# Attention kernel on one core: the parts of a projected chunk go through DRAM, and a batch's weighted sums all stand ahead of the next batch's first value tile

## The reference

```python
q, k, v = X @ Wq, X @ Wk, X @ Wv            # heads of 64; rotary embedding on q and k
att = softmax(causal(50 * tanh(q @ k.T * 256**-0.5 / 50)))
x = layernorm(X + (att @ v) @ Wo)
y = per_token_int8(x) @ weight.T * in_scale * w_scale + bias   # as float16
return layernorm(x + y)
```

## Time and profile before

| | us |
|---|---|
| median of 3 runs | 1504.92 (1504.58 to 1505.42) |
| the profiled execution, its own time | 1501.25 |
| its span, first to last instruction | 1499.3 |
| TensorE (PE) busy | 1322.7 |
| VectorE (DVE) busy | 1096.8 |
| ScalarE (ACT) busy | 849.1 |
| GpSimd (POOL) busy | 380.8 |

### The profile page before, as it was taken

One profiled execution on the slowest core, in us unless ns is written; L12 is line 12 of the kernel. 1 busy time (PEld: TensorE's weight loads), 2 busy tenths in 40 slices (PEclk: granted clock), 3 DMA queues, 4 the chain that ended last, 5 costly groups with the idle time before them and its releaser, 6 DMA issues.

```text
span 1499.3 us, 17504 instructions
## 1 busy us (share of the span) xinstructions
PE 1322.7 (88%) x5824; PEld 963.7 (64%) x5840; DVE 1096.8 (73%) x1367; ACT 849.1 (57%) x952; POOL 380.8 (25%) x448
## 2 busy tenths in 40 slices
PE   6479999978988999897886999999599799999695
PEld 5357777656655777675664777767476477777463
DVE  4369888863677888885486888888258788888485
ACT  4167687752236777764223777687123577779232
POOL 2231111102552111110265112111036312111165
PEclk9789999989988999998998999999799899999896
DMA  7766445474513454547341454446642154343541
GB/s 280 261 205 160 103 129 144 113 211 123 156 50 87 115 139 109 155 96 244 95 133 47 98 137 117 103 144 186 181 123 78 56 137 103 102 110 103 149 109 42
DMA packets 120765, 196.22 MB, mean 131 GB/s; under 512 B 26466, under 2 KB 68964, under 8 KB 116836
## 3 DMA queue, kind: packets, MB, share of 16 engines
q1 hardware_dynamic: 114916, 185.14, 44.2%
q10 hardware_dynamic: 5760, 9.97, 2.0%
HBM read 89.39 MB, written 38.54 MB: 85 GB/s over the span
## 4 chain that ended last, share of the span: by engine, by line
PE 62%; DVE 10%; DMA 9%; SPq 7%; issue 5%; ACT 3%; POOL 3%; ACTq 1%; DVEq 0%; POOLq 0%
PE ps L735 21%; PE ps L655 15%; PE ps L709 14%; PE ps L777 6%; PE ps L677 4%; SPq L427 4%; DMA y_scratch<-sums 3%; DMA rows<-r_scratch 2%; DVE prob_hi L1109 1%; ACT probs L914 1%; DVE stats L1195 1%; DVE probs L1174 1%; DMA qk<-work_r 1%; DMA r_scratch<-inverse 1%; POOL rstd L1332 1%
## 5 line engine op out<-in xcount | busy, mean ns | idle before, releaser
L735 PE MATMUL ps<-prob_hi,v 128*65 128x512 f32 (+3 forms) x1280 | 415.1, 374 | 3.3 <-DVE prob_lo L1113 3.3
L914 ACT ACTIVATE probs<-ps 128x1024 f32<-128x1024 f32 x288 | 293.6, 1020 | 161.9 <-PE ps L709 159.2
L709 PE MATMUL ps<-qk 128*128 128x512 f32 (+1 forms) x1280 | 322.9, 379 | 54.2 <-DMA qk<-work_r 28.4
L1113 DVE TENSOR_TENSOR prob_lo<-probs,prob_hi 128x1024 fp32r<-128x1024 f32 x288 | 360.1, 1250 | 9.9
L1317 POOL TENSOR_SCALAR_AFFINE_SELECT probs<-probs 128x256 f32<-128x256 f32 (+1 forms) x192 | 145.3, 765 | 808.0 <-ACT probs L919 808.0
L919 ACT ACTIVATE probs<-probs 128x1024 f32<-128x1024 f32 x288 | 305.6, 1061 | 8.8
L709 PEld LDWEIGHTS ps<-qk 128*128 128x128 f32 x1280 | 230.1, 193 | 116.9 <-ACT probs L914 27.9
L655 PE MATMUL ps<-xT,w_ring 128*128 128x512 f32 x1152 | 293.5, 399 | 10.0 <-DVE xT L1051 8.0
L1109 DVE CAST prob_hi<-probs 128x1024 fp32r<-128x1024 f32 x288 | 206.3, 716 | 118.5 <-POOL probs L1317 69.6
L655 PEld LDWEIGHTS ps<-xT,w_ring 128*128 128x128 f32 x1152 | 219.6, 193 | 58.3 <-DVE xT L1051 9.3
L735 PE MATMUL ps<-prob_lo,v 128*65 128x512 f32 (+1 forms) x640 | 239.2, 374 | 0.0
(11 more groups left out here) (77 smaller groups left out, 1042.9 us busy)
## 6 DMA issues: line engine op xcount, KB each, us to landing
qk<-work_r SPq DMA_DIRECT2D x256, 128.0 KB, 2.3
qk<-work_r SPq DMA_DIRECT2D x488, 64.0 KB, 2.0
y_scratch<-sums SPq DMA_DIRECT2D x128, 130.0 KB
wo<-wo_scratch SPq DMA_DIRECT2D x8, 2048.0 KB, 7.8
y_raw<-y_scratch SPq DMA_DIRECT2D x64, 256.0 KB, 4.1
w_ring<-w_scratch SPq DMA_DIRECT2D x15, 1024.0 KB, 5.8
x_raw<-X_T SPq DMA_DIRECT2D x16, 512.0 KB, 5.1
x_in<-X SPq DMA_DIRECT2D x32, 256.0 KB, 2.9
```

Of the source, the lines that this page charges most:

```text
L709: mm = nc.tensor.matmul(scores[:, g % 2, col:col + REP * w].rearrange("p (h q) -> p h q", h=REP), qk[:, n % 2, i, 2 + part, keys], qk[:, n ...
L735: mm = nc.tensor.matmul(sums_ps[:, :, GQ - w:GQ], v[:, kt, v0:v0 + width], p[:, at, col:col + REP * w].rearrange("p (h q) -> p h q", h=REP ...
L914: nc.scalar.activation(probs[:, prob_place(g), :], scores[:, g % 2, :], ACT.Tanh, scale=SCORE_SCALE / SOFTCAP).then_inc(capped, 1)
L1113: nc.vector.tensor_tensor(prob_lo[:, prob_place(g), :], probs[:, prob_place(g), :], prob_hi[:, hi_place(g), :].bitcast(F32), ALU.subtract) ...
```

## The change

A part of a chunk is written by one DMA of 128 partitions (`send`) to a new DRAM tensor, and read from there into `qk` (`take`) by 4 DMAs for k and 2 for each half of q, all issued by SP. `rope_read` waits for the send alone. For m > 1 the high part is taken right behind the low part's send, the low part one step later; for m = 1 all takes stand at steps 15 to 17 of unit 0. `qk` has a new inner order, all q ahead of all k, so `score` waits for both head pairs' parts together. The weighted sums of steps 69 to 71 stand ahead of value tile 0; value tile 1 stands behind `spread_rows` of tile 0. The value weights' last two quarters are loaded at step 14. `wo` is loaded after a batch's last score, its low half behind `load_rows` of tile 1; in the last batch both halves are loaded at steps 1 and 2 of its last unit, into the place of xT. ScalarE issues no puts.

```diff
--- before
+++ after
@@ -101,6 +101,8 @@
+    chunk_scratch = nc.dram_tensor("chunk_scratch", [2, 3, 2, P, T], F32, kind="Internal").ap()
...
@@ -123,8 +125,9 @@
-        qk = sb("qk", [P, 2, 2, 4, T], F32R)
-        wo = over("wo", "qk", [P, 2, KO, C], F32R, skip=32 * KB)
+        qk = sb("qk", [P, 2, 2 * REP + 4, T], F32R)
+        wo_first = over("wo", "qk", [P, 2, KO, C], F32R, skip=32 * KB)
+        wo_last = over("wo_last", "xT", [P, 2, KO, C], F32R)
...
@@ -309,8 +313,11 @@
-        def puts_upto(m):
+        def k_puts_upto(m):
...
+        def q_puts_upto(m):
+            return 64 * (m // 2 + 1)
...
@@ -324,9 +331,9 @@
-        def wait_put(eng, m, x):
-            for i in range(2):
-                eng.wait_ge(k_put[m % 2][i] if x == 0 else q_put[m % 2][x - 1][i], puts_upto(m))
+        def wait_sent(eng, m, x):
+            for low in range(2):
+                eng.wait_ge(chunk_sent[place_of(m, x)][low], 16 * ((3 * m + x) // 2 + 1))
...
@@ -334,6 +341,9 @@
+        def wo_of(b):
+            return wo_last if b == B - 1 else wo_first
...
@@ -395,37 +405,6 @@
-        def put(eng, m, x, low):
-            eng.wait_ge(rope_lo if low else rope_hi, chunks_upto(m, x))
-            if m == 0:
-                eng.wait_ge(w_stored[1], 16)
-                eng.wait_ge(w_stored[2], 16)
-            if m == 1:
-                eng.wait_ge(wo_stored, 32)
-            if m >= 2:
-                eng.wait_ge(scored, unit_scored(m - 2))
-            if m % UB == 1 and m > 1:
-                eng.wait_ge(o_done, rows_upto(m // UB - 1, NT - 1))
-            buf = qk[:, m % 2, :, :, :]
-            for i in range(2):
-                if x == 0:
-                    for half in range(2):
-                        src = work_r[64 * half + 32 * i:64 * half + 32 * (i + 1), place_of(m, x), 1 - low, :].bitcast(F32)
-                        for copy in range(2):
-                            r0 = 64 * copy + 32 * half
-                            eng.dma_start(buf[r0:r0 + 32, i, 2 + low, :].bitcast(F32), src
-                                         ).then_inc(k_put[m % 2][i], 16)
-                else:
-                    cols = slice((x - 1) * HT, x * HT)
-                    for r in range(REP):
-                        h = REP * i + r
-                        for half in range(2):
-                            src = work_r[32 * h:32 * (h + 1), place_of(m, x), 1 - low, half * HT:(half + 1) * HT].bitcast(F32)
-                            r0 = 64 * low + 32 * half
-                            eng.dma_start(buf[r0:r0 + 32, i, r, cols].bitcast(F32), src
-                                         ).then_inc(q_put[m % 2][x - 1][i], 16)
...
@@ -486,6 +465,13 @@
+            def load_wo(b, part):
+                if b == B - 1:
+                    sp.wait_ge(projected, chunks_upto(U - 1, 2))
+                sp.dma_start(wo_of(b)[:, part, :, :].rearrange("p k n -> p (k n)").bitcast(F32),
+                             wo_scratch[:, part * KO * C:(part + 1) * KO * C]
+                             ).then_inc((wo_hi_loaded, wo_lo_loaded)[part], 16)
...
@@ -494,6 +480,40 @@
                 cols = slice(part * KC * C // 2, (part + 1) * KC * C // 2)
                 sp.dma_start(w_v[:, :, :, :].rearrange("p w k n -> p (w k n)")[:, cols].bitcast(F32),
                              wv_scratch[:, cols]).then_inc(wv_loaded, 16)
+
+
+            def send(m, x, low):
+                sp.wait_ge(rope_lo if low else rope_hi, chunks_upto(m, x))
+                if m >= 2 and x == 0:
+                    sp.wait_ge(k_put[m % 2], k_puts_upto(m - 2))
+                elif m >= 2:
+                    sp.wait_ge(q_put[m % 2][x - 1], q_puts_upto(m - 2))
+                sp.dma_start(chunk_scratch[m % 2, x, low], work_r[:, place_of(m, x), 1 - low, :].bitcast(F32)
+                             ).then_inc(chunk_sent[place_of(m, x)][low], 16)
+
+            def take(m, x, low):
+                sp.wait_ge(chunk_sent[place_of(m, x)][low], 16 * ((3 * m + x) // 2 + 1))
+                if m == 0:
+                    sp.wait_ge(w_stored[1], 16)
+                    sp.wait_ge(w_stored[2], 16)
+                if m == 1:
+                    sp.wait_ge(wo_stored, 32)
+                if m >= 2:
+                    sp.wait_ge(scored, unit_scored(m - 2))
+                if m % UB == 1 and m > 1:
+                    sp.wait_ge(o_done, rows_upto(m // UB - 1, NT - 1))
+                for half in range(2):
+                    if x == 0:
+                        src = chunk_scratch[m % 2, 0, low, 64 * half:64 * (half + 1), :].rearrange("(i d) n -> d i n", i=2)
+                        for copy in range(2):
+                            r0 = 64 * copy + 32 * half
+                            sp.dma_start(qk[r0:r0 + 32, m % 2, 2 * REP + 2 * low:2 * REP + 2 * low + 2, :].bitcast(F32), src
+                                         ).then_inc(k_put[m % 2], 16)
+                    else:
+                        src = chunk_scratch[m % 2, x, low, :, half * HT:(half + 1) * HT].rearrange("(h d) n -> d h n", d=32)
+                        r0 = 64 * low + 32 * half
+                        sp.dma_start(qk[r0:r0 + 32, m % 2, 0:2 * REP, (x - 1) * HT:x * HT].bitcast(F32), src
+                                     ).then_inc(q_put[m % 2][x - 1], 16)
             def put_sums(b, j, c):
                 n = groups_upto(b, j, c)
@@ -533,11 +553,13 @@
             sp.wait_ge(w_lo_done, 1)
             sp.dma_start(wo_raw[:, :, :], Wo.rearrange("(k p) n -> p k n", p=P)).then_inc(wo_raw_in, 16)
             for x in range(3):
-                put(sp, 0, x, 0)
+                send(0, x, 0)
                 if x == 0:
                     sp.wait_ge(projected, chunks_upto(0, 0))
                     load_wk(1)
-                put(sp, 0, x, 1)
+                send(0, x, 1)
+                take(0, x, 0)
+                take(0, x, 1)
             sp.wait_ge(projected, chunks_upto(0, 2))
             load_wq(1)
@@ -552,21 +574,31 @@
                         if m == 1 and s == 5:
                             sp.wait_ge(wo_hi_done, 4)
                             sp.dma_start(wo_scratch[:, 0:KO * C],
-                                         wo[:, 0, :, :].rearrange("p k n -> p (k n)").bitcast(F32)
+                                         wo_first[:, 0, :, :].rearrange("p k n -> p (k n)").bitcast(F32)
                                          ).then_inc(wo_stored, 16)
                             sp.wait_ge(wo_lo_done, 4)
                             sp.dma_start(wo_scratch[:, KO * C:2 * KO * C],
-                                         wo[:, 1, :, :].rearrange("p k n -> p (k n)").bitcast(F32)
+                                         wo_first[:, 1, :, :].rearrange("p k n -> p (k n)").bitcast(F32)
                                          ).then_inc(wo_stored, 16)
                         if s == 3 and m % UB and m + 1 < U:
                             sp.wait_ge(projected, chunks_upto(m, 0))
                             load_wk(m + 1)
                         if u == UB - 1 and s == 14:
                             load_div(b, 0)
+                            if b + 1 < B:
+                                load_wv(b + 1, 2)
+                                load_wv(b + 1, 3)
                         if at := chunk_at(b, u, s, turns(u, 5, 10, 14)):
-                            put(sp, *at, 0)
-                        if (at := chunk_at(b, u, s, turns(u, 6, 11, 15))) and at != (UB * b + UB, 2):
-                            put(sp, *at, 1)
+                            send(*at, 0)
+                        if at := chunk_at(b, u, s, turns(u, 6, 11, 15)):
+                            send(*at, 1)
+                            if m > 1:
+                                take(*at, 0)
+                        if (at := chunk_at(b, u, s, turns(u, 7, 12, 16))) and m > 1:
+                            take(*at, 1)
+                        if m == 1 and s >= 15:
+                            take(1, s - 15, 0)
+                            take(1, s - 15, 1)
                         if s == turns(u, 0, 0, 12)[2] and m < U:
                             sp.wait_ge(projected, chunks_upto(m, 2))
@@ -582,32 +614,28 @@
                             load_x_turned(b + 1, s - 12)
                             if s == 15:
                                 load_wq(m + 1)
-                        if u == UB - 1 and m < U and s in (14, 15):
-                            load_wv(b + 1, s - 12)
-                        if u == UB - 1 and s == 11:
-                            sp.wait_ge(scored, scores_upto(b, u * 2 * NS + NS - 1))
-                            sp.dma_start(wo[:, 0, :, :].rearrange("p k n -> p (k n)").bitcast(F32),
-                                         wo_scratch[:, 0:KO * C]).then_inc(wo_hi_loaded, 16)
+                        if b == B - 1 and u == UB - 1 and s in (1, 2):
+                            load_wo(b, s - 1)
                         if u == UB - 1 and s == 17:
```

(35 more changed lines are left out.)

9 lines of the change are left out of this document (5 added, 4 removed).

## The result

The changed kernel takes 1532.4 us (median of 4 runs, 1528.98 to 1534.38) against 1505.17 for the kernel before (1504.58 to 1507.07): a ratio of 1.0176, interval 1.0152 to 1.02. **It is slower by 27 us; the forecast was 16 us faster.** Its profiled execution took 1528.98 us and is compared with the 1501.25 of before; the spans are 1526.9 and 1499.3.

The account below looks back on a forecast made before the run. PE bounds the attention stretches, so time could come only from its stops. +12.1 (unit 1) - 7 (start) - 16 (boundaries) - 5.2 (last batch) = -16.1 us: 1485.1 profiled, 1489 as median; range 1475 to 1503.

Parts of the forecast that it names:

- Prices: Assumed costs: 0.63 us per back-to-back SP issue, 2.6 us for a send's landing, 2.9 us for a take's.
- Part 1: Attention stretches: chunk 2's low part reaches step 2 of the next unit with 2.1 us cover; worth 0.
- the round trip misses the deadline: Slower rival: at step 2 of the next unit, 11 times, landings exceed the 2.1 us cover: 23 us, 1512; chance 0.1.
- Part 2: Unit 1, once: late takes stop PE for 9.9 us, plus 2.2 at low clock; loss 12.1, ends 6 and 15.
- Part 3: Start of the kernel: chunks 1 and 2 arrive earlier for PE's first scores; gain 7 us, ends 4 and 9.
- Part 4: Three batch boundaries: SP's chain to the reciprocal loads moves 4.3 us earlier; gain 5.3 us each, 16 in all.
- the boundary gives nothing: Rival: wo's low half 5 us late, or the send slow under value-weight loads; boundaries give 0 to 2 each, 1502; chance 0.12.
- Part 5: End of the last batch: wo loaded early, so the second reciprocal load comes 5.2 us earlier; ends 3 and 6.
- the boundary gives all: Rival: SP's chain does not hold spread_rows(1), so 9.21 + 2.2 us goes at each boundary: 1471; chance 0.08.
- The bounds of the sum: Whole kernel: 1478 (start 9, boundaries 7 each less what cannot coincide) to 1499 (unit 1 at 15, boundaries at 3).

Follow-up runs that it names:

- extra sends: Kernel before, with every part also sent to DRAM (96 sends, 50 MB, unread) ahead of its puts, VectorE waiting for the landing: 1534.32 us, ratio 1.0187.
- the copies: Kernel before, with 84 copies of 512 KB DRAM to DRAM ahead of the puts, which only the next such copy waits for: 1517.31 us, ratio 1.0081.
- the two best kernels: Kernel before, direct puts, rest of change, SP's reciprocals earlier: 1472.18 us; changed kernel with unit 1's takes, last units' loads, reciprocals and wo's low half reordered: 1490.81 us.

## Why the prediction was wrong

**The step that failed is Prices.** It charged a take 0.63 us on SP and 2.9 us of landing, from rows of other transfers, and let takes overlap without limit. The runs put 1.17 us of all DMA engines in its place, and landings of up to 9.34 us for a send and 10.74 for a take where other transfers are ahead. The row to see it in was there: eight of k's puts, 128 KB each onto 32 partitions, in 5.03 us are 208 GB/s. SP looked like their limit, and the transfers were at theirs just below. The DMA view of the kernel before, 58 to 82 us in 40 slices, shows it:

```profile
DMA  4000289999999896999999875434444444444443
GB/s 147 0 0 0 55 184 205 212 219 219 212 219 205 116 184 218 410 287 219 219 328 287 266 219 133 99 96 109 109 109 109 109 109 109 106 109 102 106 106 92
```

While k's puts run, the engines are 0.8 to 0.9 busy at 205 to 219 GB/s. From 75 us on the puts are q's, of 64 KB each; SP issues 32 of them back to back in 21.60 us, and the engines are 0.4 busy at about 109: these SP did hold. So for k the cut in issues removed only the outer of two limits of nearly the same size. For q it removed the real one, but the sends now stand in series (9.34 and 7.08 us in the chain at the start). Part by part:

- **Part 1, deadline of step 2.** The cover of 2.1 us is small, as stated. In the units inside the batches (2, 5, 6, 9, 10, 13, 14) no stop came. In units 3, 7 and 11 the loads of x and q weights share the engines: at 279.40 a send lands in 5.09 and the take behind it in 8.50 us, 13.6 against the 9.4 at which I had said that it decides. With these loads moved behind the takes the three stops fell to 1.3 us and less. Together with unit 15, where two 2 MB loads of wo are issued at 1385.91, right behind the takes, this is +18 us; in unit 15 they were not moved, so that they are the cause there is not shown. The rival "the round trip misses the deadline" named the place rightly; it was priced for 11 units at 2.1 us and came in 4 at 3 to 6. I gave it 0.1, on the ground that its rows were of crowded moments. The deadline lies in such moments.
- **Part 2, unit 1.** The mechanism is confirmed by moving the takes: the stop goes. Its size was off. Twelve takes by 1.17 us are 14 us; from 144.68 that is 158.7, and if the last one needs some 2 us more to land, an estimate from the 64 KB puts of before (2.0 in all), 160.7, against 161.85. The four takes of chunk 2 move beside them. The stop is 16.2 us, not 9.9, and the whole loss 19.4, not 12.1.
- **Part 3, the start.** Wrong in sign: +3.0, not -7. I let chunk 1's send land 2.6 us after its issue. It took 9.34, behind chunk 0's eight takes, and the first score came at 85.47 instead of 79.52.
- **Part 4, the boundaries.** -6.4 in all, not -16. The first inverse was to be stored 4.3 us earlier. It is at 361.83 against 335.27, 26.6 later. The last low part was ready at 349.41 against 323.24, 26.2 later, so from there to the store it is 12.4 us against 12.0: nothing gained. The send that precedes it took 6.91 us and not 2.6. This is the rival "the boundary gives nothing", by the second cause that it named, the send under the value-weight loads; wo came late by 1.2 us at most. The order of PE's work showed no worth while SP holds the reciprocals; the part had said that PE gains nothing by being early. One reading in it was wrong: the eight puts ahead of the last value weights, 319.76 to 324.93, are those of chunk 2's high part. Its low part, ready only at 323.24, is put by ScalarE.
- **Part 5, the last batch.** Right in its mechanism: PE's 9.83 us stop is 4.07, and the store of sums no longer stands in the chain. The size is -6.7 against -5.2, a little past the end of 6.
- **The rival "the boundary gives all".** Its 1471 was for a kernel in which SP's chain does not hold the reciprocals. The changed kernel is not that one. With direct puts and SP reordered 1472.18 was measured, and by the starts of ACT each boundary there gives 11.6 to 13.0 us, against the rival's 9.21 + 2.2. That the totals agree to 1 us is chance all the same: that kernel has neither unit 1's loss of 12.1 nor the start's gain of 7.

The bounds of the sum were loose as well: a start of 9 and boundaries of 7 each give 1482, not 1478. It does not bear on the miss.

What stays open is why extra sends cost 18 us more than the copies, beyond the 8 in units 0 and 1, and how much of the 19 us between the two best kernels is traffic.

## What to carry to other kernels

When a change replaces many small DMAs by few large ones, work out the rate behind the old issues first: bytes over issue time. If that is near what those partitions take in, the issues were hiding the transfer, and fewer of them buy nothing; if the engines are half idle behind them, as with q's puts here, the issues were the limit. Price a new transfer by the busiest moment in which it has a deadline, with the bytes ahead of it in the queue, not by the median of a row; and after each stop removed, look for the next load in line before counting the gain.

## What the runs showed of the hardware

- Onto 32 partitions the transfers of this kernel move about 225 GB/s (takes) and 205 to 219 (k's puts) with nearly every DMA engine busy, from or to 128 partitions about 400 to 416.
- A 512 KB send takes 2.95 us with no take ahead of it and 9.34 behind eight takes of 256 KB. The Trainium skill ("DMA: Bandwidth & Descriptors", Anatomy of one DMA) has, for DMAs that GpSimd issues, a fixed 2.0 us plus the bytes over 436 GB/s, which makes an estimate of 3.2 us. For these sends, which SP issues, the trace is near it for the send alone and not behind others.
- SP issues a take (DRAM to 32 partitions) in 0.43 us where it is not held (four in 1.71 at 324.84), a put from SBUF in 0.63.
- Some 44 MB of traffic that nobody waits for cost 12 us (8 to 16), although the DMA engines' share in an attention stretch had been only 0.49. The loss arose at the batches' ends, where PE waits for loads; inside the batches it was nothing.
